# Product-key similarities from the tokens' Gram matrix with scale and keys in one weight, and a first layer without a load stage

## What is computed

```python
x = _layernorm(x + _L1_xattn_ref(...))        # the norm ahead: stage s4norm
# _L1_ffn_ref: H = 8, KD = 128, NUM_KEYS = 64, TOPK = 8
q = jnp.einsum('bnd,de->bne', x, w_q)         # 256 -> 2048 columns
mean = jnp.mean(q, axis=(0, 1))
var = jnp.var(q, axis=(0, 1))
q = (q - mean) * jax.lax.rsqrt(var + BN_EPS) * bn_gamma + bn_beta
q = q.reshape(b, n, 2, H, KD).transpose(2, 0, 1, 3, 4)
sim = jnp.einsum('pbnhd,hkpd->pbnhk', q, keys)
sx, ix = jax.lax.top_k(sim[0], TOPK)
sy, iy = jax.lax.top_k(sim[1], TOPK)
```

## Time and profile before

| | us |
|---|---|
| median of 3 runs | 2629.89 (2623.74 to 2634.03) |
| the profiled execution, its own time | 2615.49 |
| its span in the trace | 2613.7 |
| PE busy | 2245.9 (86% of the span) |
| DVE busy | 1705.5 (65%) |
| ACT busy | 961.5 (37%) |
| POOL busy | 852.7 (33%) |
| load stage and wait for `W` | 0 to 14.4 |
| `s4norm`, to the next stage's first matmul | 1851.5 to 1872.85 |
| `sides` | 1872.85 to 2058.3 |
| `ex` | 2058.3 to about 2600 |

### The profile page before, as it was taken

The page is one execution under the profiler, slowest core; times in us unless marked ns, Lnnn a source line. Parts: engine busy times, 40 slices in busy tenths (PEclk is TensorE's granted clock), DMA queues, the critical chain, the costliest instruction groups (busy, mean ns, idle before and its releaser), DMA issues. The chain is left out here.

```text
span 2613.7 us, 34978 instructions
## 1 busy us (share of the span) xinstructions
PE 2245.9 (86%) x12808; PEld 1537.1 (59%) x12808; DVE 1705.5 (65%) x4406; ACT 961.5 (37%) x1900; POOL 852.7 (33%) x471
## 2 busy tenths in 40 slices
PE   7788888998964994998995787879699889999997
PEld 2355555634654993465563444336466678888886
DVE  5799999515653126464147996541488788888886
ACT  2398898315846212055312432032123322222220
POOL 0198888004508954052011332431200111111110
PEclk9899999999987996999997888989799899999999
DMA  3121111000023662101000000020300000000001
GB/s 97 38 81 49 49 51 39 11 0 1 1 104 125 224 226 75 35 2 40 0 21 19 1 1 1 1 79 1 129 1 1 3 1 1 1 1 1 1 1 33
DMA packets 57902, 101.02 MB, mean 39 GB/s; under 512 B 7874, under 2 KB 39490, under 8 KB 56452
## 3 DMA queue, kind: packets, MB, share of 16 engines
q1 hardware_dynamic: 56196, 94.59, 10.8%
q0 software_dynamic: 1536, 4.20, 0.5%
HBM read 88.94 MB, written 9.57 MB: 38 GB/s over the span
## 5 line engine op out<-in xcount | busy, mean ns | idle before, releaser
L749 POOL TENSOR_TENSOR XT<-mamba_DU,scan_BS 128x1024 f32<-128x1024 f32 x128 | 299.1, 2361 | 156.3 <-DMA scan_BS<-mamba_rows 118.5
L878 DVE TENSOR_TENSOR_SCAN scan_H<-scan_AB,XT 128x512 f32<-128x512 f32 x256 | 296.2, 1208 | 8.5 <-POOL XT L749 5.0
L2488 PE MATMUL ex_HP<-XT,pe_DOWN 128*128 128x256 f32 x1024 | 246.5, 387 | 7.1 <-PEq L2334 6.3
L2519 PE MATMUL ex_OP<-pe_UP,ex_GH 128*128 128x256 f32 x1024 | 231.5, 380 | 0.0
L2549 ACT ACTIVATE ex_GH<-ex_HP 128x512 f32<-128x512 f32 x128 | 76.5, 599 | 379.3 <-PE ex_HP L2488 344.6
L763 PEld LDWEIGHTS scan_TP<-ident,scan_H 128*128 128x128 f32 x1024 | 120.1, 142 | 157.9 <-DVE scan_H L878 81.3
L808 ACT ACTIVATE scan_AB<-mamba_E,mamba_AA 128x510 f32<-128x510 f32 x256 | 198.7, 776 | 38.4 <-DVE scan_H L878 34.1
L2488 PEld LDWEIGHTS ex_HP<-XT,pe_DOWN 128*128 128x128 f32 x1024 | 192.0, 192 | 31.9 <-issue 6.4
L2519 PEld LDWEIGHTS ex_OP<-pe_UP,ex_GH 128*128 128x128 f32 x1024 | 194.0, 190 | 26.0
L772 PE MATMUL scan_YT<-mamba_BC,ident 128*128 128x512 f32 x384 | 198.5, 599 | 4.1 <-ACT scan_YS L824 2.3
L763 PE MATMUL scan_TP<-ident,scan_H 128*128 128x128 f32 x1024 | 147.6, 278 | 46.5 <-DVE scan_H L878 46.5
(11 more groups left out here) (417 smaller groups left out, 4639.5 us busy)
## 6 DMA issues: line engine op xcount, KB each, us to landing
moe_W<-in_L_ffn_w SPq DMA_DIRECT2D x32, 1024.0 KB, 7.5
scan_BS<-mamba_rows SPq DMA_DIRECT2D x64, 256.0 KB, 3.1
pe_DOWN<-in_L_ffn_down SPq DMA_DIRECT2D x1, 4096.0 KB, 13.4
pe_UP<-in_L_ffn_up SPq DMA_DIRECT2D x1, 4096.0 KB, 22.8
moe_dispatch<-s4t_BOTH SPq DMA_DIRECT2D x1, 2560.0 KB, 8.7
experts_XE<-moe_dispatch SPq DMA_DIRECT2D x16, 160.0 KB, 2.4
moe_answers<-experts_YE SPq DMA_DIRECT2D x16, 160.0 KB, 3.2
XT<-in_xT SPq DMA_DIRECT2D x1, 2048.0 KB, 7.4
```

What stands on the lines that cost most here:

```text
L749: pool.tensor_tensor(BU[:, r % 2, cs], tokens(DU, cs, r // DS), row, ALU.mult).then_inc(bu_ready, 1)
L878: v.tensor_tensor_scan(H[:, r % 2, c], AB[:, n % 2, :], BU[:, r % 2, c], 0.0, ALU.mult, ALU.add).then_inc(h_ready, 1)
L2488: ins = pe.matmul(HP[:, n % 2, a, :], DOWN[:, k, 2 * q + a, :], XT[:, k, b * BLK:(b + 1) * BLK], start=(k == 0), stop=(k == KD - 1))
L2519: ins = pe.matmul(OP[:, m % 2, 0:D], GH[:, b % 2, j, a * P:(a + 1) * P], UP[:, j, :], start=(j == 0), stop=(j == J2 - 1))
```

## The change

Three parts.

**Start.** There is no load stage. The first block issues `W`, then the first quarter of `XT` (512 tokens), `ident`, the small weights, then the other three quarters, `WO` and `X`. PE waits for the quarter that it is about to use.

**`s4norm` becomes `norm_gram`.** Beside the norm, POOL subtracts one row (the mean of the first 128 tokens) from each normed tile into `XC` (eight instructions of two tiles), with a column of ones behind it, and PE accumulates `XC^T [XC 1]` over the 16 tiles: two f32 matmuls of 258 columns a tile, each six tiles behind its transposition. ACT copies the result, divided by T, to `GS`.

**`peer_sides`.** The variance of each query column c is read from the Gram matrix: PE multiplies `GS` with the chunk's weights (`spread`, two matmuls of 258 columns), DVE multiplies with the transposed weights `WQT` and sums over the row in one instruction (`accumulate`), 16 times in all. In four groups g of CG = 4 chunks, POOL multiplies the keys with the scale (`scale_keys`), PE folds keys and query weights into one weight (`fold`, `turn`), ACT copies it to `WP`; the shift becomes a bias row, which POOL splits into three bfloat16 parts (`split_bias`, a chain of six instructions on 3 partitions x 256). The similarities are then one product of `XT` with `WP`: a unit (g, u) is two tiles of 128 tokens times the 256 key columns of a group, four f32 matmuls and two bfloat16 ones for the bias (`sims`), 32 units in all, three of them in PSUM (BANKS). DVE scans a unit with eight MAX8 and eight FIND_INDEX8 (`scan`). `WQT` adds a load of 2 MB, issued with the others two stages earlier.

```diff
-        stage_load(nc, io, X, XT, ident, with_x=stage_mamba not in stages)
+        if stage_mamba not in stages:
+            stage_load(nc, io, X, XT, ident, with_x=True)
...
                         sp.dma_start(W[:], io["L0_attn_in_projT"].rearrange("(k p) n -> p k n", p=P)).then_inc(w_loaded, 16)
-                        sp.dma_start(WO[:], io["L0_attn_out_projT"].rearrange("(k p) n -> p k n", p=P)).then_inc(loaded, 16)
+                        sp.dma_start(*first_group(io, XT, 0)).then_inc(xt_loaded[0], 16)
+                        sp.dma_start(ident[:], io["ident"]).then_inc(loaded, 16)
...
+                        for g in range(1, NG):
+                            sp.dma_start(*first_group(io, XT, g)).then_inc(xt_loaded[g], 16)
+                        sp.dma_start(WO[:], io["L0_attn_out_projT"].rearrange("(k p) n -> p k n", p=P)).then_inc(wo_loaded, 16)
...
                         for g in range(NG):
+                            pe.wait_ge(xt_loaded[g], 16)
...
-        norm_only(nc, "s4norm", X, X, XT, ident, base=Z)
+        norm_gram(nc, "s4norm", X, Z, XT, ident, FO, next_inputs.GS)
...
+                for t in range(NT + LAG):
+                    if t < NT:
+                        turn(t)
...
+                    if t >= LAG:
+                        ins = gram(t - LAG)
...
+    ACCUMULATE_TO, SCALE_AT, FOLD_AT, TURN_AT, SPLIT_AT = CG, CG, 5, 6, 6
...
+                def sims(g, u):
+                    n = g * UN + u
+                    if n >= BANKS:
+                        pe.wait_ge(sims_read, n - BANKS + 1)
+                    if u == 0:
+                        pe.wait_ge(turned_copied, g + 1)
+                        pe.wait_ge(bias_split, g + 1)
+                    keys = slice(g * CK, (g + 1) * CK)
+                    for a in range(TU):
+                        t = u * TU + a
                         for k in range(KD):
...
+                            pe.matmul(SP_[:, n % BANKS, a, :], XT[:, k, t * P:(t + 1) * P], WP[:, k, keys], start=(k == 0), stop=False)
+                        ins = pe.matmul(SP_[:, n % BANKS, a, :], ONE16[0:3, :], BR[0:3, keys], start=False, stop=True)
+                    ins.then_inc(sims_ready, 1)
...
+                for c in range(2 * CG):
+                    spread(c)
+                fold(0)
+                turn(0)
+                pe.wait_ge(ones_ready, 1)
+                for g in range(NGR):
+                    for u in range(UN):
+                        sims(g, u)
+                        if g + 2 < NGR and u < ACCUMULATE_TO:
+                            spread((g + 2) * CG + u)
+                        if g + 1 < NGR and u == FOLD_AT:
+                            fold(g + 1)
+                        if g + 1 < NGR and u == TURN_AT:
+                            turn(g + 1)
...
+                    v.tensor_copy(QM[:, c, :], AT[:, c % 2, D:GW_])
+                    v.scalar_tensor_tensor(JUNK[:, c % 2], AT[:, c % 2, 0:D], 1.0, WQT[:, c, :], ALU.mult, ALU.mult,
+                                           accum_out=VAR[:, c:c + 1]).then_inc(at_read, 1)
...
+                def split_bias(g):
+                    b, x, h = B0[0:3, g % 2, :], BX[0:3, :], BH[0:3, :]
+                    pool.wait_ge(bias_copied, g + 1)
+                    for n in range(2):
+                        ch.link(pool.tensor_copy(h, b if n == 0 else x))
+                        if n == 0:
+                            ch.link(pool.tensor_scalar(x, h, SPLIT[0:3, 0:1], None, ALU.mult))
+                            ch.link(pool.tensor_tensor(x, b, x, ALU.subtract))
+                    ch.link(pool.tensor_scalar(b, h, SPLIT[0:3, 1:2], None, ALU.mult))
+                    pool.tensor_tensor(BR[0:3, g * CK:(g + 1) * CK], x, b, ALU.subtract).then_inc(bias_split, 1)
+                    pool.wait_ge(bias_split, g + 1)
...
+                for g in range(NGR):
+                    for u in range(UN):
+                        keep(g * UN + u)
+                        if g + 2 < NGR and u == SCALE_AT:
+                            scale_keys(g + 2)
+                        if g + 1 < NGR and u == SPLIT_AT:
+                            split_bias(g + 1)
```

352 lines of the change are left out of this document (281 added, 71 removed).

## The result

The changed kernel takes 2594.0 us (median of 4 runs, 2588.2 to 2596.7) where the kernel before, beside it, took 2632.0 us (median of 4, 2623.7 to 2635.7): 38.0 us less. The forecast was 2598 us, from 2576 to 2616. The profiled execution took 2596.7 us, its span is 2594.9 us.

What follows compares the result with a forecast made beforehand. PE was taken to bound `sides`, with DVE at 76% behind it, and a chain of transfers the start. Start -7.0, norm +14.4 and sides -39.6 sum to -32.2 us: 2598 us against the median, range 2576 to 2616.

Steps and rivals of the forecast that it cites:

- Start, -7.0: First loads: `W` issued at about 0.7 us, PE starting at 7.3 instead of 14.37; -7.0 us, from -4 to -8.
- Rival 5: Start: `W` and the quarter arrive no sooner relative to the first instruction; takes back 3 us at most; no chance given.
- Norm, +14.4: `s4norm`: transpositions and Gram steps fill PE in one stretch to 1884.9; +14.4 us, lower end +6, upper +17.
- Sides, -39.6: `sides`: DVE's 64 statistics go, scans of 32 units set the pace; 145.2 us against 184.8, -39.6.
- a boundary: `sides`, between groups: DVE waits 6.7 us for POOL's late bias and PE's slow first unit; three make 20.1 us.
- units in which fold and turn meet a low clock: `sides`, scan: 3 us added for units where PE's fold and turn meet a low clock.
- DVE is the bound: `sides`, scan: a unit takes PE 1.95 us, 0.9 less than DVE's 2.84, so DVE sets the pace.
- The skill's rule: POOL's `split_bias`: one-input instructions at roughly line rate, some 0.36 us each; split 3.2 us, sum 6 us lower.
- 1 (quick POOL, warm PE): `sides`: casts and scalars near 0.30 us, `split_bias` 3.0, PE restarts at full clock; 2580 us; chance 0.20.
- 2 (slow POOL): `split_bias`: all six POOL instructions take 1.40 us, 3.9 more in four places, +16; 2614 us; chance 0.12.
- 3 (PE and DVE close): `sides`: clock falls in units with fold and turn, DVE waits some 3 us more a group; 2608 us; chance 0.11.
- 4 (low clock throughout): Scan and Gram steps: brief idles keep PE at 1.2 GHz, slower than before, +26; 2656 us; chance 0.04.

Runs made afterwards that it cites:

- e1: The kernel before with only the start changed (tokens by groups, no load stage); 2606.8 us where before took 2614.4, ratio 0.9970.
- e6: The changed kernel with half of the norm's Gram product left out for 14 of 16 token tiles; 2590.8 us (one run), before 2631.0.
- e7: The changed kernel with POOL's row subtraction in the norm cut to 2 of 256 columns; 2587.1 us (one run), before 2631.0.
- e10: e5 with POOL's apply of the next group put between a group's two subtractions in the norm; 2547.9 us, before 2615.3, ratio 0.9748.
- e8: The changed kernel without the 64 small bf16 matmuls that add the bias; 2583.1 us (one run), before 2631.0.
- e5: The changed kernel with fold, turn, split behind units 2, 3, 3 and the head of the sides reordered; 2551.6 us, before 2614.4, ratio 0.9762.
- e3: The changed kernel with the bias split one unit earlier, behind unit 5 and not 6; 2569.7 us, before 2614.4, ratio 0.9826.
- e9: The changed kernel with the first three steps of the bias split done three times over; 2610.4 us (one run), before 2631.0.

## Why the prediction was right, step by step

The sum was -32.2 us; stage by stage the traces of chip C give -7.0 + 13.6 - 43.1 + 1.0 (untouched stages) = -35.5. The sign held in each of the three parts, and the mechanism in all but one point: in the units beside a spread it is TensorE and not DVE that sets the pace.

**Start, -7.0.** Measured -7.3 at the convolution and -7.0 at the first scan. PE began at 7.66 for a forecast of 7.3, ACT 9.7 us behind the issue of `W` for 9.36 + 0.4. Right in its steps. Rival 5 (nothing gained) is out by e1.

**Norm, +14.4.** Measured +13.5. The full stretch of PE, from tile 5 to the last Gram step, took 19.1 us for a forecast of 20.7, and began 0.7 us later. PE was full and set the end (e6), a Gram step was four records in 0.87 us as in the earlier trace rows, POOL's subtraction 1.25 to 1.34 for 1.25, the two copies 0.66. What the working did not name is PE's 1.83 us wait for POOL in the second group (e7, e10).

**Sides, -39.6.** Measured -43.1. Term by term:

| term | forecast | measured |
|---|---|---|
| ahead of the first scan | 23.0 | 22.0 |
| `split_bias` | 4.8 | 4.5 |
| scan of a unit on DVE | 2.84 | 2.78 |
| what an accumulate adds between two scans | 0.65 | 0.63 (0.41 in e8, where DVE sets the pace) |
| accumulates and statistics between scans, in all | 8.2 | 8.2 |
| a unit on PE, full clock | 1.95 | 2.44 beside a spread, 2.54 alone |
| idle of PE at a boundary | 7 | 5.0, 5.0, 4.9 |
| first unit behind a wait | 3.9 | 4.2 (head), 4.7 (boundary) |
| a boundary | 6.7 | 6.8, 6.8, 6.7 |
| three boundaries with the units behind them | 20.1 | 22.5 |
| units in which fold and turn meet a low clock | 3 | 0 |
| PE's share of DVE's work in the scan | 80% | 98% (91.9 of 93.9 in e5) |

The boundary came out right out of two errors: the bias was ready 2.1 us behind the run-dry DVE, as reckoned, but the first unit took 4.7 and not 3.9, and my 0.6 for signals and the second unit did not lie in it. The 32 units at 2.78 are 1.9 us below the forecast, the added 3 us did not appear, and the head was 1.0 lower, 5.9 in all; the boundaries with their second units took 2.4 of it back, which leaves the 3.5 us. The accumulate came out right by luck too: 0.41 of its 0.63 are DVE's own work and 0.22 are the wait for TensorE, which the sum had nowhere.

**The term that was mis-sized** is the small matmul: half of a 256-column f32 record, 0.11, was taken from no row of its kind, and it costs 0.36 between f32 matmuls. The step "that is 0.9 less than DVE" was wrong; it was 0.24 to 0.34 less, and over a group, with spreads of 0.98 us, fold and turn, PE has about as much to do as DVE. So "DVE is the bound" holds for the units without a spread only. What this cost is read from e8. Behind a wait the first unit took 3.6 us at the head and 3.4 at the first boundary there, where after had 4.2 and 4.7. All 64 small matmuls together are worth 7.4 us of the stage, and the part that the forecast did not have (0.25 of each 0.36) some 5 us, by an estimate in proportion. The time came out right all the same, since the terms above were about as much too high.

**The skill's rule.** POOL's cast of 256 columns took 0.39 us, near the 0.36 that I had estimated by the Trainium skill, "GPSIMD Engine Reference", section 4.1, for a one-input instruction; the TENSOR_SCALAR took 0.92, far from it. The whole split was 4.5 us, where the values that I took gave 4.8 and the estimate by the rule 3.2. The assumption that POOL's time goes by columns and not by partitions held: a TENSOR_TENSOR of 256 columns took 0.71 us on 3 partitions and 0.73 on 128.

**The rivals.** 1 (quick POOL, warm PE): the cast was quick, the clock was not; e5 shows that PE does restart at the full clock behind an idle of 1.68 us. 2 (slow POOL): out, 4.5 us. 3 (PE and DVE close): they were close. The only waits inside a group are 2.00 and 0.30 us in the second unit behind two of the boundaries, at the low clock, and the 0.22 us in the units beside a spread; the 3 us a group that it named did not come. 4 (low clock throughout): the clock was 0.89 from the first unit on, with the rows at half standing behind the four long waits.

**The level of the forecast.** The difference was taken from the median and not from the profile, 14 us lower. That was right, since the changed kernel of the result has the long combine stage; but I had no reason for it then beyond the median. From the profile's level the same difference would have given 2583.3, inside the range as well.

## What to carry to other kernels

When a slow chain on a side engine gates the first unit of the next group, look at the place where that chain is queued before looking at its length: here the split one unit earlier, a change of one number, was worth 10 us, and fold, turn and split behind units 2, 3 and 3 were worth 21 us, over half of what the whole change had brought. Made longer where it stood, the chain cost its full added length at every boundary. Order the work at the head of a stage so that the first group's chain does not queue behind the second group's; here the shorter idle of PE was paid back a second time, in its clock (1.6 us). Where no wait is listed, compare the distance between two starts with the sum of the other engine's work: here it was 3.41 us on both sides, and showed which engine set the pace. Compare traces stage by stage: an untouched stage differed by 17 us between executions, half of the effect to be measured.

## What the runs showed of the hardware

- A bf16 matmul of 3 rows and 256 columns between f32 matmuls takes 0.36 us of PE's time (0.28 in the record; 0.21 to the next start, and 0.15 in the mean by which the four f32 records of its tile are longer), more than one and a half times an f32 record of the same columns (0.215).
- The granted clock behind an idle of PE: behind 1.68 us of idle (e5) a tile of four records took 1.10 us and the next ones stayed there, and so behind 1.46 us (e3, third boundary); behind 2.27 us (e3, first boundary) the first tile took 1.10 and the second 2.08, and behind the same 2.27 us at the second boundary 1.50 and 2.08; behind 4.75 to 5.04 us (after) the first already took 2.04. So the length of the idle alone does not fix it. 1.1 is the level of 2.4 GHz (granted clock 1.00 from 1893.96 to 1896.47 in e5), 2.1 that of 1.2 GHz (0.50 from 1945.97 to 1950.60 in after).
- DVE's applies of the norm were slowed by POOL's two-input subtraction beside them. Three took 1.22, 2.00, 1.27 and 3.09 us in the four groups of after; with the subtraction cut to two columns (e7) the last three read:

```profile
1864.34 1.22 DVE L2359 TENSOR_SCALAR X<-X,s4norm_MV,s4norm_RS 128x256 f32<-128x256 f32 x3
1868.65 1.22 DVE L2359 TENSOR_SCALAR X<-X,s4norm_MV,s4norm_RS 128x256 f32<-128x256 f32 x3
1869.99 1.06 DVE L2359 TENSOR_SCALAR X<-X,s4norm_MV,s4norm_RS 128x256 f32<-128x256 f32 x3
```

  POOL's own one-input apply (1.40 us), which runs beside DVE's in the first group, slows nothing (1.22). The Trainium skill, "SBUF — State Buffer", section "Who interferes with whom", says that the two engines share one pair of ports and that it is locked, so that of two instructions that use it one blocks while the other works. The rows agree for the two-input subtraction, which kept its 1.25 to 1.34 us while DVE lost up to 1.9: of the three applies from 1878.36 on, the two beside a subtraction took 1.49 and 1.36 us, the third 0.40.
- The combine stage, the same in every kernel here, took 35 to 37 us on chips A and C and 54.5 to 54.7 us on chip B; the changed kernel had 54.4 in the profile of the result, with PE's issue stalling 40 times, and 35.2 on chip C. Its cause stays open. Another untouched stretch, from the first `tkproj_ring` to the first `cv_XF`, took 292.6 us in after and in before, and 286.2 to 286.6 in e1 and e7 to e9. The mean granted clock in it was 0.83 in before and after and 0.86 in e1 and e7, with the same instructions. The trace of e1 is of its quickest run, 7.5 us under its median, and this stretch alone is 6.3 us shorter there; so one trace can stand some microseconds off its kernel's median in a stretch that nobody touched. What raises the clock there is open too.
